# A Mamba-2 scan's chunk buffer released by its last reader, the dt chain moved forward, and four runs of constant matmuls on TensorE

## What is computed

```python
zxbcdt = x @ in_w.T                       # z 512, xBC 768, dt 8 columns
xBC = silu(conv1d(xBC, 4 taps) + conv_b)  # xs (8 heads x 64), B (128), C (128)
dt = softplus(dt + dt_bias); dA = exp(dt * A)
h = h * dA_t + dt_t * xs_t (x) B_t        # over 1024 steps
y_t = h . C_t + D * xs_t
y = rmsnorm(y * silu(z), gnorm_w) @ out_w.T
# then: token memory, cross attention, routing to 8 experts, their two matmuls
```

## Time and profile before

| | us |
|---|---|
| runs, not profiled: median of 3 | 702.9 (701.93 to 703.07) |
| the profiled execution's own time | 705.62 |
| its span, first to last instruction | 703.9 |
| TensorE busy | 603.1 (86%) |
| VectorE, ScalarE, GpSimd busy | 385.1, 326.0, 169.9 |
| mean granted TensorE clock | 0.927 |

### The profile page before, as it was taken

The page is one execution under the profiler, slowest core; times in us unless marked ns, Lnnn a source line. Parts: engine busy times, 40 slices in busy tenths (PEclk is TensorE's granted clock), DMA queues, the critical chain, the costliest instruction groups (busy, mean ns, idle before and its releaser), DMA issues.

```text
span 703.9 us, 13775 instructions
## 1 busy us (share of the span) xinstructions
PE 603.1 (86%) x4690; PEld 475.3 (68%) x4691; DVE 385.1 (55%) x945; ACT 326.0 (46%) x709; POOL 169.9 (24%) x190
## 2 busy tenths in 40 slices
PE   1999966877777879999869999999629999999995
PEld 0454434666666755656558888888519999999994
DVE  3686663656666657636345555556464444444541
ACT  1587985465555453124455666654412323232320
POOL 0200003555555541064200000000121232222311
PEclk9999987899998899999689999999858999999998
DMA  7000113344444149000340000000470111010110
GB/s 252 20 1 0 45 65 104 113 142 137 135 141 127 61 130 410 11 3 1 101 139 9 17 17 17 17 17 18 117 229 18 31 37 37 28 39 30 35 21 0
DMA packets 49322, 50.53 MB, mean 72 GB/s; under 512 B 7606, under 2 KB 43674, under 8 KB 49274
## 3 DMA queue, kind: packets, MB, share of 16 engines
q1 hardware_dynamic: 43930, 44.70, 19.8%
q0 software_dynamic: 2208, 5.14, 2.7%
q10 hardware_dynamic: 3136, 0.07, 0.3%
HBM read 39.24 MB, written 5.26 MB: 63 GB/s over the span
## 4 chain that ended last, share of the span: by engine, by line
PE 66%; DVE 11%; DMA 10%; ACT 5%; issue 4%; SPq 3%; POOL 1%; ACTq 0%; DVEq 0%; POOLq 0%
PE banks L2131 12%; PE banks L2142 11%; PE banks L1626 8%; DMA arena<-arena 7%; PE banks L1989 4%; SPq L378 3%; PE banks L2014 2%; PE banks L1965 2%; PE banks L2019 2%; DVE arena L1148 2%; PE banks L2032 2%; PE banks L2028 2%; PE banks L1895 2%; PE banks L1671 2%; DVE ybuf L1387 1%
## 5 line engine op out<-in xcount | busy, mean ns | idle before, releaser
L2142 PE MATMUL banks<-arena,prob_b 128*128 x368 | 83.1, 379 | 0.0
L992 ACT ACTIVATE prob_b<-banks,gate_w 128x128 f32<-128x128 f32 x92 | 26.3, 369 | 118.8 <-PE banks L2131 118.8
L2131 PE MATMUL banks<-ybuf 128*128 128x128 f32 x560 | 80.8, 280 | 0.0
L2131 PEld LDWEIGHTS banks<-ybuf 128*128 128x128 f32 x560 | 74.4, 197 | 1.1
L2142 PEld LDWEIGHTS banks<-arena,prob_b 128*128 128x128 f32 x368 | 68.2, 190 | 8.4
L1626 PE MATMUL banks<-featT,ybuf 128*128 128x512 f32 x160 | 72.7, 612 | 0.9 <-ACT featT L647 0.9
L1387 DVE TENSOR_REDUCE ybuf<-banks 128x12 f32<-128x1848 f32 (+1 forms) x32 | 46.2, 1442 | 21.2 <-PE banks L1989 21.1
L1626 PEld LDWEIGHTS banks<-featT,ybuf 128*128 128x128 f32 x160 | 30.9, 197 | 38.7 <-issue 36.9
L1111 DVE SCALAR_TENSOR_TENSOR arena<-arena,conv_w 128x512 f32<-128x512 f32 x72 | 49.0, 746 | 14.0 <-ACT arena L661 13.9
L471 POOL TENSOR_TENSOR arena<-arena 128x1024 f32<-128x1024 f32 x16 | 37.7, 2356 | 69.1 <-ACT arena L733 60.7
L611 POOL DMA_INDIRECT out<-featT,dts x23 | 23.4, 1016 | 122.8 <-DVE featT L1574 122.8
(11 more groups left out here) (345 smaller groups left out, 1266.9 us busy)
## 6 DMA issues: line engine op xcount, KB each, us to landing
arena<-cum_rows SPq DMA_DIRECT2D x16, 512.0 KB, 4.9
arena<-W1T SPq DMA_DIRECT2D x8, 1024.0 KB, 13.6
arena<-W2T SPq DMA_DIRECT2D x8, 1024.0 KB, 11.5
arena<-arena SPq DMA_DIRECT2D x16, 384.0 KB, 3.6
featT<-ecum_rows SPq DMA_DIRECT2D x30, 128.0 KB, 3.1
xres<-x SPq DMA_DIRECT2D x4, 512.0 KB, 11.1
x_rows<-xres SPq DMA_DIRECT2D x16, 128.0 KB, 2.3
ybuf<-attn_in_wT SPq DMA_DIRECT2D x1, 1288.0 KB, 7.1
```

Source lines behind the costliest of these rows:

```text
L992: i = act.activation(hidT[:, p, f, :], bank[2 * p + 1][:, (f - 4) * P:(f - 3) * P], ACT.Relu, bias=b1_cols[:, ds(e * NFF + f, 1)])
L2131: m = pe.matmul(bank[2 * p + half][:, f * P:(f + 1) * P], w1_now[k][p][:, (4 * half + f) * P:(4 * half + f + 1) * P], xsT[:, p, k, :], sta ...
L2142: m = pe.matmul(bank[4 + p][:, 0:D], hidT[:, p, f, :], w2_of[:, ds(e * NFF + f, 1), :].rearrange("p a n -> p (a n)"), start=(f == 0), stop ...
```

## The change

It does five things. `xbc` holds five blocks of a chunk instead of six: C is read by TensorE straight from `xbcT`, so the buffer's last reader is the B by C matmul, and the next load into it waits for `g_mm` instead of `inter_mm`; the load stands ahead of `cum` and `ecum` in SyncE's body. `norm_w` gets the semaphore of the weights, so ScalarE's first square roots wait for no small load; the wait for the other six stands before the first projection is emptied. The dt chain's steps stand earlier in all three programs. The memory weights are turned inside the projections (item `n`), and chunk 0's clamp follows there. `keep_busy` puts matmuls of the constants `ones` and `ident` into a bank that nobody reads, at four places.

```diff
-        xbc = cut([2, NX, P])
+        xbc = cut([2, NZ + 1, P])
...
-                    + in_block(2)[:4] + [("e", 0)] + in_block(2)[4:]
-                    + in_block(3)[:4] + [("c", 0)] + in_block(3)[4:])
+                    + in_block(2)[:1] + [("e", 0)] + in_block(2)[1:]
+                    + [("c", 0)] + in_block(3)[:8] + [("n", 0)] + in_block(3)[8:])
...
                 if wait:
-                    sp.wait_ge(S("inter_mm"), used)
-                sp.dma_start(xbc[:, p, :, :], xbcT[:, :, ds(first, P)]).then_inc(S(f"chunk_loaded{p}"), 16)
+                    sp.wait_ge(S("g_mm"), used)
+                sp.dma_start(xbc[:, p, :, :], xbcT[:, 0:NZ + 1, ds(first, P)]).then_inc(S(f"chunk_loaded{p}"), 16)
...
                 for p in range(2):
+                    load_chunk(2 * i + p, p, True)
                     load_cum(2 * i + p, p, True)
                     load_ecum(2 * i + p, p, True)
-                    load_chunk(2 * i + p, p, True)
...
-            for dst, src in ((norm_w[:, :], a["attn_norm_w"]),
-                             (gnorm_w[:, :], a["attn_gnorm_w"]),
+            act.dma_start(norm_w[:, :], a["attn_norm_w"]).then_inc(S("w_loaded"), 16)
+            for dst, src in ((gnorm_w[:, :], a["attn_gnorm_w"]),
...
-            act.wait_ge(S("small_loaded"), 16 * 7)
             row_sd(1, range(0, 4))
-            act.wait_ge(S("past_cleared"), 1)
+            act.wait_ge(S("w_loaded"), 32)
+            act.wait_ge(dve_once, at("past_cleared"))
...
                 if kind == "x":
+                    if n == 0:
+                        act.wait_ge(S("small_loaded"), 16 * 6)
                     keep_x(n)
...
-                if (kind, n) == ("x", NX * 2 + 5):
+                if (kind, n) == ("x", NX * 2 + 3):
                     soft_plus()
+                if kind == "n":
+                    keep_nat()
+                    act.wait_ge(dve_once, at("cum_kept"))
+                    act.wait_ge(S("conv_sum"), NX * (NBLK - 1))
+                    act.wait_ge(S("past_kept"), NX * (NBLK // 2))
+                    clamp(0, 0, False)
...
-                if p == 2 * PAIRS:
+                if p == 2 * PAIRS - 1:
                     dt_raws()
+                if p == 3 * PAIRS - 2:
+                    dt_steps()
                 if p == 3 * PAIRS - 1:
-                    dt_steps()
-                if p == 3 * PAIRS + 1:
                     decays()
...
+            def keep_busy(b, count):
+                for _ in range(count):
+                    pe.matmul(bank[b][:, 0:P], ones[:, :], ident[:, :], start=True, stop=True)
+
+            keep_busy(7, 16)
+            pe.wait_ge(S("w_loaded"), 32)
...
-                pe.matmul(bank[1][:, P:2 * P], xbc[:, p, NZ, :], xbc[:, p, NZ + 1, :], start=True, stop=True
+                pe.matmul(bank[1][:, P:2 * P], xbc[:, p, NZ, :], xbcT[:, NZ + 1, ds(t * P, P)], start=True, stop=True
...
+            keep_busy(5, 12)
             for n in range(4):
                 turn_y(n)
...
             route(NT - 1)
 
+            keep_busy(2, 16)
             pe.wait_ge(dve_once, at("hot_ready"))
...
             m.then_inc(pe_once, reached("found_mm"))
+            keep_busy(2, 24)
             pe.wait_ge(dve_once, at("block_expert_ready"))
```

More of the change, by code:

```diff
@@ L684, in soft_plus, with keep_nat, clamp, decay_matrix @@
                 act.activation(dt_exp, dt_exp, ACT.Ln, bias=1.0).then_inc(act_once, reached("dt_ln"))
-            act.wait_ge(S("small_loaded"), 16 * 7)
+            def keep_nat():
+                act.wait_ge(pe_once, at("nat_turned"))
+                act.activation(w_nat[0:SD, :, :].rearrange("p a n -> p (a n)"), in_bank("n", 0)[0:SD, :], ACT.Copy).then_inc(act_once, reached("nat_kept"))
+            def clamp(t, p, wait):
+                act.wait_ge(S(f"cum_loaded{p}"), 8 * (t - p) + 16)
+                if wait:
+                    act.wait_ge(S("intra_mm"), t - 1)
+                for h in range(H):
+                    i = act.activation(lmat[:, p, h, :], cum_all[:, p, h, :], ACT.Relu, bias=cum[:, ds(t * H + h, 1)], scale=-1.0)
+                i.then_inc(S("clamped"), 1)
+            def decay_matrix(t, p):
+                act.wait_ge(S("clamped"), t + 1)
+                act.activation(lmat[:, p, :, :], lmat[:, p, :, :], ACT.Exp, scale=-1.0).then_inc(S("decay_mat"), 1)
             row_sd(1, range(0, 4))
-            act.wait_ge(S("past_cleared"), 1)
+            act.wait_ge(S("w_loaded"), 32)
+            act.wait_ge(dve_once, at("past_cleared"))
             for kind, n in IN_ORDER:
@@ L1681, in _ @@
             summ, q_nat = w_nat[0:SD, 0, :], w_nat[0:SD, 1, :]
-            pe.wait_ge(S("mem_w_loaded"), 16 * 9)
-            for i, w in enumerate((summ_w, mem_q_w)):
-                for k in range(KD):
-                    m = pe.transpose(bank[4][0:SD, i * D + k * P:i * D + (k + 1) * P], w[:, k, :], ident[:, :])
-            m.then_inc(pe_once, reached("nat_turned"))
             pe.wait_ge(act_once, at("nat_kept"))
@@ L1711, in mix @@
                 for k in range(NZ):
-                    m = pe.matmul(INTER_BANK[p][:, k * P:(k + 1) * P], state[:, k * P:(k + 1) * P], xbc[:, p, NZ + 1, :], start=True, stop=True)
+                    m = pe.matmul(INTER_BANK[p][:, k * P:(k + 1) * P], state[:, k * P:(k + 1) * P], xbcT[:, NZ + 1, ds(t * P, P)], start=True, stop=True)
                 m.then_inc(S("inter_mm"), 1)
```

60 lines of the change are left out of this document (28 added, 32 removed).

## The result

| | before | after |
|---|---|---|
| runs, median (lowest to highest) | 702.99 us (701.93 to 703.48) | 681.86 us (680.71 to 684.65) |
| profiled execution, time | 705.62 us | 682.72 us |
| its span | 703.9 us | 681.0 us |
| mean granted clock | 0.927 | 0.947 |

The ratio is 0.9707, with a 95% interval of 0.9674 to 0.9741. So the changed kernel is about 21 us faster by the medians, and 22.9 us by the two spans. The forecast was 679.4 us within 673.5 to 687.

The account below looks back on a forecast made before the run. It took the chunk's transfer to bound the loop, small-load waits the head, and TensorE the stretch between; 23.5 us off the profiled 705.62 gives 682.1, less 2.7 to the median 679.4 us, range 673.5 to 687.

Parts of the forecast that it names:

- a second chain without a transfer: Loop: add_state, gate, square, exp, make_m, decay_state closes once a chunk and remains, step 8.02 us instead of 8.84.
- Both chains that I called slack: Loop: the chunk's transfer has 2 to 7 us in hand, the clamp behind keep_out 2 us to spare.
- The head: Start to projections: first projection 6.7 us earlier, its first 32 records 2.9 us shorter at the later rate; 9.6 us.
- The cover for x's last part: Head: statistics of x's late last part cost nothing, hidden by TensorE's eight banks; without that 1 to 3 us.
- The rival that the constants do nothing for the projections: Head: projections still start at half rate despite the constants, 682.3 us; chance 0.12.
- The passage: Between projections and loop: turned weights and clamp moved ahead of the last z, everything after 1.5 us earlier.
- The loop's load: Loop: chunk's transfer, issued earlier, leaves the chain; 13 steps of 0.82 us give 10.7 us.
- The loop's end: Last chunk, with no transfer ahead: 0.4 us gained, bounded by VectorE's own order.
- y: After the loop: twelve constants let the 16 turns run faster, 0.9 us gained; at half rate 0.7 to 2.5 lost.
- Router: Router: first 16 constants lose 1.4 us, the later 24 gain 1.8 net; together 0.4 gained.
- The sum: Whole kernel: 9.6 + 1.5 + 10.7 + 0.4 + 0.9 + 0.4 = 23.5 us saved.
- the 2.7 as a constant offset: Whole kernel: profiled execution stands 2.7 us above the runs' median, so profiled 682.1 us means 679.4 us.

Follow-up runs that it names:

- head_alone: Kernel before with only the head's waits changed, no constants: 699.15 us, ratio 0.9915.
- no_head_constants: Changed kernel without the 16 constant matmuls in the head, the other three places kept: 686.88 us, ratio 0.9735.
- wait_back: Changed kernel with the chunk's load in its new place but waiting for `inter_mm` again instead of `g_mm`: 684.64 us, ratio 0.9711.
- place_back: Changed kernel with the chunk's load put back behind its `cum` and `ecum` loads, the new wait kept: 690.13 us, ratio 0.9780.
- loop_end_constants: Changed kernel with 10 more constant matmuls ahead of the last chunk's inter product: 682.09 us, ratio 0.9668.
- loop_alone: Kernel before with only the load's new place and wait, five blocks, and C read from `xbcT`: 693.88 us, ratio 0.9840.
- no_constants: Changed kernel without the constant matmuls at any of the four places: 688.41 us, ratio 0.9769.
- all_three: Changed kernel plus constants at passage and loop's end; router's first 16 dropped, 18 instead of 24 in its second run: 677.48 us, ratio 0.9596.
- no_first_router_constants: Changed kernel without the 16 constants ahead of the router's running sum, the later 24 kept: 681.68 us, ratio 0.9674.

## Why the prediction was right

**What bounds the kernel.** The reading that a second chain without a transfer closes on itself at 8.02 us held best of all: 8.00 in the changed kernel and 8.00 in all ten siblings with the new order. Both chains that I called slack stayed slack: the turn is never waited for, and ScalarE idles 0.2 to 2.1 us ahead of its square, for VectorE's gate. I had counted 2 for every step, which was too much for some.

**The head.** Both terms were right: 6.7 (6.71) and 2.9 (2.72; 2.76 by the run without its constants, 1.5 to 2.8 by all profiles). That 6.71 hits so well is in part luck: the square root came at 6.78 and not at 6.43, and the 9.02 of the first turn and the 2.41 behind it stand for 9.2, the worst case of the constants, and 2.2. The two are independent: head_alone has the first without the second. The cover for x's last part held. The rival that the constants do nothing for the projections is refuted by no_head_constants.

**The passage.** 1.5 forecast, 2.47 measured. The start was right, as the first product came at 92.86, 1.9 earlier than the head's shift alone, forecast 1.6. The part behind it was taken as unchanged; it was 0.6 shorter here because the full rate came back at 100 us, and 1.0 longer in another execution. So this term is right within a spread that I had not given it.

**The loop's load.** 10.7 forecast, 11.0 measured. The cause, however, is the place in the queue (0.60 of the 0.85 us a step) and not the new wait, which I had not separated; wait_back and place_back separate these two. The other 0.25 I had taken as nothing; that it comes of the smaller transfer is argued only. By the figures that the Trainium skill (DMA: Bandwidth & Descriptors, Anatomy of one DMA) gives, a transfer of 64 KB less would be 0.15 us shorter, an estimate. That section gives them for transfers that GpSimd issues, and SyncE issues these. The trace does not agree: the median to landing fell by 0.4, from 3.6 to 3.2.

**The loop's end.** This is the step that failed: "0.4, bounded by VectorE's own order". VectorE's order was not the bound. Timelines of TensorE, before and then after:

```profile
245.28 1.14 PE L1712 MATMUL banks<-arena 128*128 128x128 f32 x8
246.35 1.09 PE L1716 MATMUL banks<-arena 128*64 128x128 f32 x16
247.38 1.12 PE L1719 MATMUL banks<-arena 128*128 128x512 f32 x2
```

```profile
221.83 1.20 PE L1730 MATMUL banks<-arena 128*128 128x128 f32 x8 [2.97 <-DVE arena L1174]
222.96 1.98 PE L1734 MATMUL banks<-arena 128*64 128x128 f32 x16
224.87 1.75 PE L1737 MATMUL banks<-arena 128*128 128x512 f32 x2
```

The faster loop leaves TensorE idle for 2.97 us ahead of the last inter product, where before it had come straight from other work, and the last products then take 1.98 and 1.75 us instead of 1.09 and 1.12. It cost 1.0 us instead of gaining 0.4, and 2.2 in the executions in which the lower level began earlier. loop_end_constants shows it: the same place without that idle stretch takes 4.88. There VectorE's order is the bound, as forecast, but it is 0.70 longer than I had counted, by the gate. Without that it would be some 4.2 against 4.64 before, which is the forecast 0.4. So two terms were missing, TensorE's half rate and behind it the long gate; the first is shown by a run, the size of the second is an estimate.

**The constants later.** y: 0.9 forecast, 0.88 measured; but in loop_alone, without constants, the turns ran at full rate by themselves, and the same distance was 10.51 against 11.06 here and 11.94 before. Router: −1.4 and +1.8 forecast, −1.2 and +1.35 in the changed kernel (+1.84 without the 16 ahead of them). That they end late at both places was right, and the price was right within the spread of executions. By the prediction's own 0.22 us a matmul at full rate, the ends at half rate would be 9.4, 515.4 and 10.7 and not 9.2, 515.1 and 10.3; neither the sum nor the range hangs on it.

**The sum.** 23.5 forecast against 22.9 in the profiled executions. The median fell 21.1, since the profiled execution of the kernel before stood 2.7 above its median and that of after only 0.9. I had carried over the 2.7 as a constant offset; it is a single execution's distance and not a property of the kernel, and it makes most of the 2.5 us by which I forecast too low.

The Trainium skill (TensorE: Matmul & The Clock Gate, Part 1) holds that such a ramp is under 1% of a typical kernel's span and not worth fitting to a count. Each one is: 2.7 us is 0.4% here. But from no_constants to all_three, which has constants at five places, the spans differ by 11.9 us, 1.7%. Some 1.9 of it lies between scorer and route, where both have the same code; the other 10.0 are 1.5%. So for a kernel with five such places the traces do not agree.

## What to carry to other kernels

A transfer's place in an in-order queue can hold it longer than its own wait does: before changing what a load waits for, look at what stands ahead of it in the queue, and issue it one round earlier if its buffer allows. When a loop gets faster, look for the engine that now idles at its end; here TensorE's new 3 us of waiting halved its rate for the products behind it. Constants in front of a wait cost what they end late, and pay if heavy work follows directly: in the router 24 ended 1.8 us late and still gained, 18 gained more, and 16 with over 4 us of waiting behind them were a plain loss. When a stall is taken away, another term can stand right behind it, as VectorE's long gate stood behind the half rate.

## What the runs showed that I had not expected

- The same instructions at the same offset can take two lengths. From the first to the second chunk's turn the nine kernels with the changed kernel's code there took between 11.3 and 12.9 us, and from chunk 14 to 15 the seven that idle 2.97 us there and have its code took 5.48 to 6.84 us. The more of the stretch was granted 0.50, the longer it took: a mean of 0.62 with 11.3 and of 0.50 with 12.9 at the first, 0.72 with 5.48 and 0.50 with 6.84 at the second. The head's records and the router's constants vary in the same way. In the profiles the first two places differ by up to 2.8 us together, so they could make most of the changed kernel's spread of 3.9 (680.71 to 684.65), which is argued and not shown. They move a comparison by more than the edits under test, which is why distances were compared.
- The granted clock reads 1.00 from 0 to 8 us in the changed kernel, while the 32 records of the constants start 0.21 us apart there until 7.6 us, and 0.11 us apart after it. In the head the length of a record tells the rate, the clock row does not; in the router the two agree.
- VectorE's gate of chunk 14 (L1186) took 1.53 us instead of 0.69 in the changed kernel and 1.39 in loop_end_constants. In nine profiles it took 1.39 to 1.55, and in each of them GpSimd's L480 (1.04 us) had started 0.03 to 0.20 us before it; it then ends 0.54 to 0.56 us behind GpSimd's end. In no_first_router_constants GpSimd starts 0.8 after it, and the gate takes 0.69. The Trainium skill (SBUF — State Buffer, Who interferes with whom) describes one port pair that the two engines take in turns, each for a whole instruction; the rows agree with that. No run here tested it alone. In the changed kernel it cost nothing on the path; in loop_end_constants it stands on it.
